# A longer split tail of the experts, early query turns, and a mask added by TensorE for five of eight score chunks

## The reference

```python
x = x + L0_xattn(layernorm(x), ctx)
x = x + L0_experts(layernorm(x))
x = x + L1_xattn(layernorm(x), ctx, seg_id)
x = x + L1_ffn(layernorm(x))

# L0_experts: 32 experts of width 96, all computed for all tokens and weighted
h = silu(x @ w_gate.T) * (x @ w_up.T)
y = y + h @ w_down.T * combine[:, e]

# L1_xattn: 16 heads of 128 + 64 rotary, keys from a 64-wide latent of 64 tokens
q_c = q @ W_dq
q_rope = rope(q_c @ W_qr)
scores = (q_nope @ k_nope.T + q_rope @ k_rope.T) / sqrt(192)
good = (k_ids <= seg_id) & (k_ids >= seg_id - 8)
attn = softmax(where(good, scores, -1e30))
out = (attn @ v).reshape(...) @ W_o
```

## Time and profile before

| | |
|---|---|
| median of three runs | 842.53 us |
| profiled execution | 842.54 us, of which the span is 840.7 us |
| PE busy | 785.3 us, 93% |
| DVE, ACT, POOL busy | 663.6, 535.7, 464.2 us |
| experts end (last gate_up) | 671.23 us from the span's start |
| first FFN matmul (the 12 of `f_front(0, 0)`) | 780.54 us |

### The profile page before, as it was taken

The page is one execution under the profiler, slowest core; times in us unless marked ns, Lnnn a source line. Parts: engine busy times, 40 slices in busy tenths (PEclk is TensorE's granted clock), DMA queues, the critical chain, the costliest instruction groups (busy, mean ns, idle before and its releaser), DMA issues.

```text
span 840.7 us, 14354 instructions
## 1 busy us (share of the span) xinstructions
PE 785.3 (93%) x4848; PEld 669.3 (80%) x4848; DVE 663.6 (79%) x1567; ACT 535.7 (64%) x1236; POOL 464.2 (55%) x782
## 2 busy tenths in 40 slices
PE   3687999999999999999899999999999999898997
PEld 3466788888888888888788878898888867577787
DVE  7789999899998989989889794865754678977634
ACT  6788877787778877788774555433332268974432
POOL 3688969779586895858855576433310004980000
PEclk9799999999999999999999999999999999899999
DMA  7000120011200121000200323968423000100001
GB/s 242 14 0 1 39 76 1 2 39 39 76 1 1 39 61 54 2 2 1 68 26 14 127 65 89 241 166 267 133 65 88 1 1 14 51 14 1 1 1 51
DMA packets 28265, 45.60 MB, mean 54 GB/s; under 512 B 3936, under 2 KB 18080, under 8 KB 28064
## 3 DMA queue, kind: packets, MB, share of 16 engines
q1 hardware_dynamic: 26800, 41.31, 16.7%
q10 hardware_dynamic: 1392, 3.37, 1.1%
HBM read 43.49 MB, written 1.18 MB: 53 GB/s over the span
## 4 chain that ended last, share of the span: by engine, by line
PE 59%; DVE 21%; ACT 11%; issue 4%; DMA 2%; POOL 1%; SPq 1%; ACTq 0%; DVEq 0%
PE PS L789 17%; PE PS L859 8%; PE PS L649 6%; PE PS L744 4%; PE PS L718 3%; PE PS L680 3%; PE PS L969 2%; DVE st L1664 2%; PE PS L701 2%; PE PS L690 2%; PE PS L671 2%; DVE yb L1566 2%; ACT P L1127 2%; DVE cat L1570 1%; DMA l_KM<-share 1%
## 5 line engine op out<-in xcount | busy, mean ns | idle before, releaser
L2272 POOL TENSOR_SCALAR raw<-raw,mvq,rsq 128x128 f32<-128x128 f32 x312 | 183.4, 602 | 1.6
L789 PE MATMUL PS<-xq,WH 128*128 128x512 f32 x472 | 148.4, 396 | 0.0
L789 PEld LDWEIGHTS PS<-xq,WH 128*128 128x128 f32 x472 | 86.3, 190 | 17.2 <-issue 1.1
L649 PE MATMUL PS<-WH,xq 128*128 128x256 f32 (+1 forms) x256 | 89.5, 368 | 7.0 <-DVE xq L1570 7.0
L789 PE MATMUL PS<-xq,WL 128*128 128x512 f32 x236 | 92.4, 392 | 0.0
L649 PE MATMUL PS<-WL,xq 128*128 128x256 f32 (+1 forms) x256 | 85.4, 352 | 0.0
L1127 ACT ACTIVATE P<-PS,sm 128x256 f32<-128x256 f32 x128 | 61.0, 497 | 25.9 <-DVE sm L1728 25.8
L859 PE MATMUL PS<-xq,m_hh 128*128 128x256 f32 x384 | 69.9, 282 | 3.1 <-ACT m_hh L1013 2.4
L1664 DVE BATCH_NORM_STATS2 st<-raw 128x6 f32<-128x128 f32 x320 | 70.5, 276 | 1.8 <-ACT raw L1099 1.8
L718 PE MATMUL PS<-PT,vr 128*128 128x256 f32 x256 | 66.4, 382 | 3.8 <-ACT PT L1013 3.8
L680 PE MATMUL PS<-kT,qT 128*128 128x256 f32 x256 | 65.9, 380 | 1.8 <-ACT qT L1116 1.8
(11 more groups left out here) (302 smaller groups left out, 2175.3 us busy)
## 6 DMA issues: line engine op xcount, KB each, us to landing
wst<-in_wgu SPq DMA_DIRECT2D x24, 256.0 KB, 3.7
l_KM<-share SPq DMA_DIRECT2D x16, 384.0 KB, 4.0
wst<-in_wall SPq DMA_DIRECT2D x18, 256.0 KB, 3.1
l_KM<-share SPq DMA_DIRECT2D x16, 256.0 KB, 5.1
dst<-in_wdn SPq DMA_DIRECT2D x24, 128.0 KB, 3.2
wst<-in_wkvx SPq DMA_DIRECT2D x8, 256.0 KB, 3.2
l_KM<-share SPq DMA_DIRECT2D x16, 128.0 KB, 4.5
m_pre<-in_wo ACTq DMA_DIRECT2D x1, 2048.0 KB, 8.7
```

Source lines behind the costliest of these rows:

```text
L649: t = e.matmul(PS[:, b, o:o + n], xq[s][:, k, c * 128:(c + 1) * 128], W[:, k, w0:w0 + n], start=(k == 0 and i == 0), stop=(k == 1 and i == 1))
L789: t = e.matmul(PS[:, b, :], W[wi][:, gu, k, :], a[:, k, cols], start=(n == 0), stop=(n == 5))
L2272: t = e.tensor_scalar(v, v, mvq[:, par, n, 0:1], rsq[:, par, n:n + 1], ALU.add, ALU.mult)
```

## The change

It has five parts.

1. `TAIL = 18`: pieces 18 to 23 are split by halves (six instead of four), and `CB` gets two more buffers in S[1] and S[2].
2. `outmix` 0 to 3, `turn` 0, 1 and `compress` 0, 1 move in between the last pieces; `queries(0, 0)` and `queries(0, 1)` come before the last two `down`. VectorE does `turn_q(0, ·)` before `settle(1)`. All cosines and sines now lie in `prea`, none in S. `turn` 2, 3 and the later queries move behind the scores.
3. For chunks 0 to 4 PE adds the mask: one bf16 matmul of an identity with the mask (broadcast over heads) in each score bank. VectorE only takes maxima from the banks, ACT reads the exponentials' input from the banks and frees them. 1/sqrt(192) goes into the copies of the keys. Chunks 5 to 7 keep a VectorE pass.
4. GpSimd does all `add_q` before the first `load_f`.
5. ACT loads the Exp and the Silu tables with two one-column activations ahead of need. `values` 2, its copy and a second buffer set for CT in `prea` move too.

```diff
-MOE = [(j, h) for j in range(20) for h in range(2)] + [(j, h) for h in range(2) for j in range(20, 24)]
+TAIL = 18
+ADDED = 5
+MOE = [(j, h) for j in range(TAIL) for h in range(2)] + [(j, h) for h in range(2) for j in range(TAIL, 24)]
...
+        if n == 46:
+            do("turn", 0)
+            do("turn", 1)
+        if n == 47:
+            do("compress", 0)
+            do("compress", 1)
         do("down", *MOE[n - 2])
+        if 41 < n < 46:
+            do("outmix", n - 42)
+    do("queries", 0, 0)
     do("down", *MOE[-2])
+    do("queries", 0, 1)
     do("down", *MOE[-1])
...
-QUERIES = {1: (4,), 2: (5,), 3: (6,), 4: (7,)}
+QUERIES = {1: (3,), 2: (4,), 3: (5,), 4: (6,), 5: (7,)}
...
+            CT = [CT, [prea[:, i, :].rearrange("p (a t) -> p a t", a=2) for i in (8, 9, 12, 13)]]
+            tqc, tqs = ([prea[:, o + n % 2, :] for n in range(16)] for o in (8, 12))
+            CB = [KM[:, z, :, :].rearrange("p a b -> p (a b)") for z in range(4)] + [S[z][:] for z in (1, 2)]
...
+                    if c < ADDED:
+                        w.wait_ge(masked, 1)
+                        t = e.matmul(PS[:, b, :], idb[:, :], mkb[:, c, :].unsqueeze(1).to_broadcast([128, 8, 64]),
+                                     start=False, stop=True, skip_group_check=True)
...
+                    b = B.at["ls", c, h // 8][0]
+                    src = PS[:, b, h % 8 * 64:h % 8 * 64 + 64] if c < ADDED else s1
+                    t = e.activation(s1, src, ACT.Exp, bias=s16[c % 3][:, 0, h:h + 1])
+                    if c < ADDED and h % 8 == 7:
+                        t.then_inc(free[b], 1)
...
+                    if c < ADDED:
+                        t = e.tensor_reduce(s16[i][:, 0, 8 * z:8 * z + 8], ps3, X, ALU.max, negate=True)
+                        continue
+                    e.tensor_tensor(S[i][:, z * 512:(z + 1) * 512].rearrange("p (h t) -> p h t", h=8), ps3,
+                                    mk[:, c, :].unsqueeze(1).to_broadcast([128, 8, 64]), ALU.add).then_inc(free[b], 1)
```

More of the change, by code:

```diff
@@ L225, in late_order @@
             do("scores", n)
-        if n == 0:
-            do("queries", 1, 1)
+        if n == 1:
+            do("turn", 2)
+            do("turn", 3)
+        for m in QUERIES.get(n, ()):
+            do("queries", m // 2, m % 2)
+        if n == 1:
             do("compress", 2)
@@ L231, in late_order @@
             do("turn_p", n - 2)
-        for m in QUERIES.get(n, ()):
-            do("queries", m // 2, m % 2)
+        if n == 7:
+            do("values", 2)
+        if n == 10:
+            do("values", 3)
         if n % 2 and n > 4:
@@ L926, in scores2 @@
                 w.wait_ge(keys_in, 4)
-                for z in range(8):
-                    emptied(("km", z))
                 for z in range(2):
+                    for y in range(4 * z, 4 * z + 4):
+                        emptied(("km", y))
                     b = fill(("ls", c, z))
@@ L1207, in place_keys @@
                 k23, o = K2[:].rearrange("p (a t) -> p a t", a=4), 32 * i
-                copy(KZ[o:o + 32, :, i % 2, :], k23[o:o + 32]).then_inc(keys_in, 1)
+                e.activation(KZ[o:o + 32, :, i % 2, :], k23[o:o + 32], ACT.Copy, scale=ROOT).then_inc(keys_in, 1)
             def early(j, h):
@@ L1383, in scalar @@
                     take_aw(3)
-            split_h(len(MOE) - 1)
[L1385 to L1391, removed]
+                if 41 < n < 46:
+                    take_bp(n - 42)
+                if n == 46:
+                    take_lt(0)
+                    take_lt(1)
+                if n == 47:
+                    take_qc(0)
+                    take_qc(1)
+            split_h(len(MOE) - 1)
             def exps2(c):
@@ L2102, in vector @@
                 if n >= MOE.index((23, 0)) + 2 and n < len(MOE):
-                    for _ in range(7):
+                    for _ in range(9):
                         next(settling, None)
@@ L2134, in scale @@
                 s3 = S[i][:].rearrange("p (h t) -> p h t", h=16)
-                w.wait_ge(exped_l.sem, exped_l.at[c])
+                if c < ADDED:
+                    for z in range(2):
+                        w.emptied(("ls", c, z))
+                else:
+                    w.wait_ge(exped_l.sem, exped_l.at[c])
                 e.tensor_reduce(s16[i][:, 1, :], s3, X, ALU.add).then_inc(dv.sem, 1)
@@ L2406, in gpsimd @@
             w.filled(("bp", 3))
-            for part in range(2, 4):
+            for part in range(2, 8):
                 add_q(part // 2, part % 2)
             w.wait_ge(downed.sem, downed.at[MOE[-1]])
-            for n in range(5):
-                for m in QUERIES.get(n, ()):
-                    add_q(m // 2, m % 2)
-                for j in FPIECES[n]:
-                    load_f(j)
+            for j in range(9):
+                load_f(j)
         def sync(e):
@@ L2509, in stage_share @@
                     n = rows.stop - rows.start
[L2510 removed]
+                    e.dma_start(CB[j % 6][rows, :], share[expert:expert + 1, :].to_broadcast([n, 1024])).then_inc(share_in[j % 6], 16)
             for z in range(2):
```

147 lines of the change are left out of this document (71 added, 76 removed).

## The result

| | before | after |
|---|---|---|
| four runs each, us | 841.06 to 845.69, median 843.69 | 859.85 to 862.56, median 861.16 |
| span of the profiled execution, us | 840.7 | 858.8 |
| mean granted clock | 0.986 | 0.979 |

The ratio of after to before is 1.0208, with a 95% interval of 1.0187 to 1.0229: the changed kernel is 17.5 us slower. The forecast said slower, by 6.2 us. The direction is right; the time lies 8 us outside the range. The profiled execution of the changed kernel took 860.84 us.

A forecast was written before the change was run, and what follows sets the result against it. PE was nearly always busy, with waits included, so at most some 11 us could be won; ACT and held banks decide the new loop. Span +3.8 and clock +2.4 take 842.54 to 848.7 us, range 843.3 to 853.0.

The forecast's parts named there:

- T +5.0: Experts' tail: T, the end of the last `gate_up`, comes 5.0 us later as `outmix` and `turn` move ahead.
- the last `gate_up` later than 677: Sign that the forecast is wrong: it would be a wait in the tail that the prediction does not see.
- CB buffers save nothing: Experts' weight buffers: two more leave the wait for piece 4's weights; cost 0, bound -1.4 to +0.5.
- T to `scores(0)` -6.8: From the last `gate_up`'s end to `scores(0)`'s end: 27.9 us before, 6.8 us shorter after.
- Exponentials 3.3, mask 0.23 each: Score chunks: sixteen exponentials from a bank take 3.3 us on ACT; each of ten mask matmuls 0.23 on PE.
- The four waits up to `project(0)`: `scores(0)` to `project(0)`: PE waits 0.95 at `scores(2)`, 2.0 and 2.3 at `values(0)`, 3.15 before `project(0)`.
- Clock +2.4, one fall: Behind the new waits up to `project(0)`: PE's granted clock falls once, costing 2.4 us.
- a second fall at project(0): Rival "Worse", chance 0.12: `project(0)`'s 6.9 us at half speed for half its length, +3.4, 852.1; or dearer masks.
- project(0) to the FFN +0.5: Last stretch before the FFN: 37.8 us of PE work plus waits; 0.5 us longer than before.
- ends near 98: hidden: `project(0)` to the FFN: GpSimd's nine `load_f` end near 98 us after the last `gate_up`, costing nothing.
- The wait for the Silu load: Before the first FFN matmul: 0.85 us, as the table load stands ahead of the split it waits for.
- the rival with waits half as long: Up to the FFN: exponentials of 3.1 and earlier DVE save about 4 us, 843 to 845; chance 0.08.

The follow-up runs named there:

- d4: Kernel before with, on TensorE alone, each next query unit issued ahead of `turn_p`; 844.80 us.
- a4: Changed kernel with the `load_f` spread between the `add_q` again and no mask added by TensorE; 852.24 us.
- a5: Changed kernel with the `load_f` spread between the `add_q` again and each late query unit one step earlier; 858.52 us.
- b2: Kernel before with only the mask of five chunks added by TensorE and their exponentials read from the banks; 851.90 us.
- d1: Changed kernel with the `load_f` spread again and `project(0)` issued later, after `values(1)` and `scores(6)`; 851.34 us.
- a1: Changed kernel with only GpSimd's order undone, the nine `load_f` again between the `add_q`; 854.17 us.
- b1: Kernel before with only GpSimd's order changed, all `add_q` first and then the nine `load_f`; 849.88 us.
- d3: Changed kernel with `load_f` spread, `project(0)` after `scores(6)`, three chunks masked by TensorE instead of five, no table touches; 846.37 us.
- e1: Changed kernel with `load_f` spread, `project(0)` after `scores(6)`, three chunks masked by TensorE instead of five, both table touches kept; 850.78 us.
- c1: Changed kernel's experts' tail and six share buffers, with orders behind `scores(0)`, masks, table loads and GpSimd's queue as before; 851.48 us.

## Why the prediction was right in direction and wrong in size

- **T +5.0: nearly right.** The same product of VectorE behind the share loads, which the change leaves alone, starts at 552.50 before and at 554.13 after; in the other kernels with this tail it starts between 550.9 and 554.0, and in d4, whose experts are those of before, at 553.4. From there to T it is 118.7 and 123.9: the tail costs 5.2 us, and 1.6 of the 6.8 is how this execution began. So the sign "the last `gate_up` later than 677" came (678.04) without a new wait in the tail.
- **CB buffers save nothing: right as far as seen.** DVE still waits 2.54 us for piece 4's weights in the row that answers to the earlier trace rows. This wait differs by execution: with six buffers from 0.21 (a4) to 3.02 (a5), with four 2.14 in b2 and 2.24 in d4; no run changed the buffers alone.

```profile
539.08 0.69 DVE L2043 TENSOR_TENSOR m_pre<-m_pre,l_S 128x512 f32<-128x512 f32 x1 [2.54 <-DMA l_S<-share]
```

- **T to `scores(0)` -6.8: right** (-6.7), with its two waits, 0.79 for a product of VectorE and 0.74 for the key banks behind the table load (0.7 and 0.75 predicted).
- **Exponentials 3.3, mask 0.23 each: right** (3.32 to 3.38, and 0.21).
- **The four waits up to `project(0)`: right** in place, cause and, within 0.7 us, in size: 1.07, 1.78, 1.66, 3.23 measured. b2 shows that the held banks can cost a wait of 8 us where the queue is another; d1, without the fourth wait, is 2.8 us faster, by intervals that just overlap.
- **Clock +2.4, one fall: too few.** The expected fall came, `values(0)` and what follows at 0.57 and 0.58, and the stretch up to `project(0)` is 1.0 us over the forecast (8.5 for 5.1 + 2.4). Then came more: `project(0)` takes 8.86 us where before it took 7.07, and `project(2)` 9.43 for 7.14. The rival "a second fall at project(0)" held, at a chance of 0.12, and cost 1.8 us of the 3.4 it was priced at. The rule on PE idling in short gaps, from the Trainium skill, "TensorE: Matmul & The Clock Gate", on psum-queue depth-cycling, cited in the prediction, was borne out here better than I weighed it. There are three low stretches where one was expected, but the third, under `project(2)`, stands behind the waits of the next point: with the loads spread it is gone.
- **project(0) to the FFN +0.5: the step that failed.** The prediction said of `load_f`: "ends near 98: hidden". It ended at T + 102.3, and PE shows no wait for it. What was not hidden was its effect on VectorE: `add_l(0)` 5.1 us longer, then waits of 3.34 and 1.90 and a clock of 0.50. I had named the risk ("if it is not, DVE's products next to it cost more"), but priced it at nothing, and looked at the large products, where the mean rises by 0.2, instead of the dependent small steps, where 0.16 becomes 1.12. a1 and b1 give its price: 7.0 and 6.2 us, of the 12.5 by which the forecast missed. By stretches of the profile, the changed kernel is over the forecast by 1.8 up to T, 0.1 to `scores(0)`, 1.0 to `project(0)` and 9.0 to the FFN. The 9.0 are mainly the wait of 3.34, 0.8 more wait at `project(2)`, and low clock in two places, 2.3 in `project(2)` and 1.8 in `project(0)`. The rest of the term was right: in a5, with the loads spread and `project(0)` at full clock, the stretch is 42.9 us, for 42.3 predicted and 41.8 before.
- The wait for the Silu load, predicted at 0.85 before the FFN, is 0.78.
- **Three sums of the prediction are slightly off**, and none of them moves the result: two thirds of 3.4 are 2.3 and not 2.4; two `keymix` of 0.95 from 13.2 end at 15.1 and not 15.35; and the rival with waits half as long comes to 842.3, outside its own 843 to 845.

Why the change loses at all, even repaired: it puts 5.2 us ahead of T, most of it work taken out of the stretch behind T, yet that stretch shrinks by only 1.1 us in d3's profile (108.2 against 109.3), and by some 2.6 if the medians are taken (d3 is 2.6 us over the kernel before). The rest comes back as 1.3 us of mask matmuls and as waits for GpSimd's sums (1.07, 1.83), ScalarE's copies (1.81, 1.26) and VectorE's products (1.74). I read this as a stretch bound by the chain over four engines and not by TensorE's work, so that little of the work moved out of it is saved. That is a reading of the waits and not shown by a run of its own. What each remaining wait of d3 would give was not tried one by one; the new order of VectorE (the first query units ahead of `settle(1)`, later ones ahead of `scale`) was never undone alone; and why the touches cost 4 us stays open.

## What to carry to other kernels

A queue that nobody waits for is not yet hidden: its operations can hold up those of another engine, here VectorE's. Before work of GpSimd is moved, look at what VectorE does in the new place, and above all for chains of tiny dependent steps. Evicting a bank early with one more pass may look like waste, but it frees the bank from the consumer's queue; ask who stands ahead of the consumer there. And before work is moved out of a stretch, check that the engine that did it sets the stretch's length.

## What was not expected of the hardware

- VectorE's steps on 128 x 2 numbers took 0.16 us alone and up to 1.13 us when they began during one of GpSimd's (1.27 us); each of these long ones ended within 0.03 us of GpSimd's end.
- It goes the other way too. After, DVE's product of 765.26 (1.23 us) starts with GpSimd's scaling, which takes 1.70 us for its usual 0.62:

```profile
765.26 1.70 POOL L2429 TENSOR_SCALAR WH<-wst 128x512 fp32r<-128x512 f32 x1
```

- The reductions of VectorE (after, 777.75 and 778.89) are not touched: 1.22 and 1.21 us beside the same loads.
- After waits of nearly one length the clock fell in one kernel and not in another: `values(0)` waits 1.81 us in d3 and 724 to 728 is granted 1.00; in e1 it waits 1.80 and the grant is 0.62. Windows of d3, then of e1:

```profile
724.00:728.00 4.00, 4.00 (x28) 1.94 (x20) 3.93 (x6) 4.00 (x16) 3.92 (x4) 1.00 0.30 84
```
```profile
724.00:728.00 4.00, 4.00 (x17) 1.34 (x10) 3.93 (x5) 4.00 (x15) 3.92 (x4) 0.62 0.28 100
```

The same at `project(2)`: behind waits of 2.44 and 2.45 it took 7.14 us in before and in d4, behind 2.45 and 2.46 it took 8.83 in c1 and in b2. Such a fall is worth 1.7 us of one execution, as much as some of the differences between kernels in the table.
